# A decoder of two layers on one core: where the four-bit stage unpacks its down weights, and when it takes a batch's mean and power

## The reference

```python
w_gu = _dequant_fp4(gate_up_packed, gate_up_scales, GROUP_SIZE)   # 2*1408 x 512
w_down = _dequant_fp4(down_packed, down_scales, GROUP_SIZE)       # 512 x 1408
gate_up = jnp.einsum('bsh,oh->bso', x, w_gu)
gate, up = (gate_up[..., :I], gate_up[..., I:])
h = jax.nn.silu(gate) * up
y = jnp.einsum('bsi,hi->bsh', h, w_down)
rms = jnp.sqrt(jnp.mean(y * y, axis=-1, keepdims=True) + EPS)
return y / rms
...
x = _layernorm(x + _L1_ffn_ref(x, ...), axis=-1)
```

## Time and profile before

| | us |
|---|---|
| median of 3 runs | 1719.92 |
| lowest and highest | 1719.76 and 1720.91 |
| the profiled execution | 1719.57 |
| its span in the trace | 1717.8 |
| PE busy | 1589.3 (93%) |
| DVE busy | 1271.8 (74%) |
| POOL busy | 740.9 (43%) |
| the four-bit stage, first matmul to end of the span | 1380.03 to 1717.8 |

### The profile page before, as it was taken

How to read it: one execution, slowest core, us unless ns; L and a number is a source line. 1 busy time by engine, 2 the same in 40 slices (tenths; PEclk the granted TensorE clock), 3 DMA queues, 4 the chain that set the end, 5 groups by cost and what they waited for, 6 DMA issues and landing times. The chain is left out here.

```text
span 1717.8 us, 26427 instructions
## 1 busy us (share of the span) xinstructions
PE 1589.3 (93%) x8812; PEld 1116.1 (65%) x8812; DVE 1271.8 (74%) x2250; ACT 941.4 (55%) x1946; POOL 740.9 (43%) x718
## 2 busy tenths in 40 slices
PE   8999998999866999998999999899898989999995
PEld 5778875666524666666667566665566767777774
DVE  6466656767879899997686784876759989767574
ACT  3222225887766676766576473664544555555642
POOL 5044164777531444444531231321132257556563
PEclk9999999999988999999999999999899999999998
DMA  6200018634030000004221121121333100000000
GB/s 220 74 1 25 1 49 219 196 104 120 2 98 1 2 1 1 1 5 131 74 76 46 57 80 41 52 70 38 88 108 94 50 1 1 0 26 25 1 25 25
DMA packets 66850, 95.73 MB, mean 56 GB/s; under 512 B 12176, under 2 KB 28688, under 8 KB 66716
## 3 DMA queue, kind: packets, MB, share of 16 engines
q1 hardware_dynamic: 60044, 81.18, 15.5%
q0 software_dynamic: 6144, 12.60, 2.8%
q10 hardware_dynamic: 528, 0.26, 0.1%
HBM read 56.25 MB, written 4.19 MB: 35 GB/s over the span
## 5 line engine op out<-in xcount | busy, mean ns | idle before, releaser
L3021 PE MATMUL bank<-fp_xT,fp_weights_values 128*128 128x512 f32 x704 | 186.1, 402 | 9.6 <-DVE fp_gate L2925 8.1
L1838 ACT ACTIVATE causal_probs<-bank,causal_neg 128x512 f32<-128x512 f32 (+3 forms) x256 | 134.3, 531 | 100.9 <-DVE causal_neg L1908 66.8
L3021 PEld LDWEIGHTS bank<-fp_xT,fp_weights_values 128*128 128x128 f32 x704 | 128.5, 188 | 55.3 <-DVE fp_gate L2925 15.7
L3048 PE MATMUL bank<-fp_wd,fp_hT 128*128 128x512 f32 x528 | 133.8, 394 | 4.8 <-DVE X L2947 3.5
L2934 DVE SCALAR_TENSOR_TENSOR fp_up<-bank,fp_weights_scales,fp_up 128x512 f32<-128x512 f32 x132 | 99.1, 751 | 44.3 <-ACT fp_up L2836 37.9
L866 DVE TENSOR_REDUCE heads_neg<-bank 128x1 f32<-128x512 f32 x128 | 86.3, 676 | 50.0 <-PE bank L917 49.9
L3048 PEld LDWEIGHTS bank<-fp_wd,fp_hT 128*128 128x128 f32 x528 | 98.5, 188 | 29.2 <-issue 6.8
L1558 PE MATMUL bank<-weights_raw,ternary_qT 128*128 128x512 bf16 x448 | 107.9, 388 | 4.9 <-DVE ternary_z L1426 2.7
L835 ACT ACTIVATE heads_probs<-bank,heads_neg 128x512 f32<-128x512 f32 x128 | 88.5, 696 | 39.4 <-DVE heads_neg L866 39.4
L1232 POOL TENSOR_TENSOR ternary_z<-ternary_z 128x1024 f32<-128x1024 f32 x16 | 37.7, 2354 | 164.4 <-DVE ternary_z L1426 164.4
L2084 PE MATMUL bank<-eye,causal_probs 128*128 128x128 f32 x640 | 101.4, 283 | 5.7 <-ACT causal_pT L1820 3.6
(11 more groups left out here) (269 smaller groups left out, 4211.4 us busy)
## 6 DMA issues: line engine op xcount, KB each, us to landing
pairs_xd<-X SPq DMA_DIRECT2D x64, 128.0 KB, 2.6
pairs_cd<-in_ctx SPq DMA_DIRECT2D x64, 128.0 KB, 2.7
causal_qS<-causal_qk SPq DMA_DIRECT2D x96, 64.0 KB, 2.9
causal_qS<-causal_qk POOLq DMA_DIRECT2D x96, 64.0 KB, 2.6
causal_kS<-causal_qk SPq DMA_DIRECT2D x96, 64.0 KB, 2.7
causal_kS<-causal_qk POOLq DMA_DIRECT2D x96, 64.0 KB, 2.4
X<-in_x SPq DMA_DIRECT2D x4, 1024.0 KB, 7.8
heads_cT<-in_ctxT SPq DMA_DIRECT2D x4, 1024.0 KB, 6.0
```

Source lines behind the costliest of these rows:

```text
L1838: act.activation(probs_of(i)[:, h + one], view[:, one], ACT.Exp, bias=neg[:, G % 2, at:at + 1], accum_out=total[:, G % 2, at:at + 1]).then ...
L3021: last = pe.matmul(banks[4 + g][:], values[:, g, n % NI, of], xT[:, part, g], start=part == 0, stop=part == 1)
L3048: last = pe.matmul(banks[t][:], hT[:, n % SLOTS, a, t * P:(t + 1) * P], wd[:, c, i], start=i == 0 and k == 0, stop=i == NI - 1 and k == 2)
```

## The change

The four instructions that unpack a block of the down weights are issued elsewhere. Block 0 is unpacked ahead of step 0, block 1 behind the last `rest` of step 2, and block `n - 1` in step `n` for n = 3 to 11, between the gate's `odd` and up's `rest`. `d_highs` goes with them: 0 behind step 0's first eviction of up, 1 at the head of step 3's evictions of up, and `n - 1` behind step n's Silu. `split(0)` stands in step 0 behind the sum, `split(n - 2)` at the head of step n for n = 3 to 12. A batch's `mean` and `invert` are issued ahead of that step's `odd` and `sum`. No instruction is added or taken away on any engine.

```diff
--- before.py
+++ after.py
@@ -2799,18 +2799,20 @@
             pool.wait_ge(norm.power_set, 1)
             for n in range(STEPS):
                 b, i = divmod(n, NI)
-                if 1 <= n <= NI:
-                    split(n - 1)
+                if 3 <= n < NI + 2:
+                    split(n - 2)
+                if b and i == 2:
+                    invert(b - 1)
                 if b and i == 5:
                     root(b - 1)
                 if n == PAST_STATISTICS + 1:
                     past.norm.root(pool, 0, B * NT - 1)
                 pool.wait_ge(gate_odd, 2 * n + 2)
                 pool.tensor_tensor(gate[:, n % 2, 0], gate[:, n % 2, 0], gate[:, n % 2, 1], ALU.add).then_inc(gate_summed, 1)
+                if n == 0:
+                    split(0)
                 if n:
                     low(n - 1)
-                if b and i == 2:
-                    invert(b - 1)
                 pool.wait_ge(up_rest, 3 * n + 3)
                 pool.wait_ge(silu_ready, n + 1)
                 pool.tensor_tensor(up[:, n % 2], up[:, n % 2], gate[:, n % 2, 0], ALU.mult).then_inc(h_ready, 1)
@@ -2867,10 +2869,14 @@
                 even(n, 2)
                 if n:
                     high(n - 1)
-                if 1 <= n <= NI:
+                if n == 3:
+                    d_highs(1)
+                first(n)
+                if n == 0:
+                    d_highs(0)
+                silu(n)
+                if 3 <= n <= NI:
                     d_highs(n - 1)
-                first(n)
-                silu(n)
                 if i == 6 and b + 1 < B:
                     act.wait_ge(past.norm.normed, (b + 2) * NT)
                 if 6 <= i < 6 + NT and b + 1 < B:
@@ -2961,17 +2967,24 @@
                                       ALU.subtract, ALU.mult).then_inc(norm.normed, 1)
 
             dve.wait_ge(weights.scaled, 1)
+
+
+            d_cut(0)
+            d_weigh(0)
             for n in range(STEPS):
                 b, i = divmod(n, NI)
+                if b and i == 2:
+                    mean(b - 1)
                 odd(n, 1)
                 odd(n, 3)
-                if b and i == 2:
-                    mean(b - 1)
+                if 3 <= n <= NI:
+                    d_cut(n - 1)
+                    d_weigh(n - 1)
                 for g in range(1, NG):
                     rest(n, g)
-                if n < NI:
-                    d_cut(n)
-                    d_weigh(n)
+                if n == 2:
+                    d_cut(1)
+                    d_weigh(1)
                 if n == PAST_STATISTICS:
                     past.norm.statistics(dve, 0, B * NT - 1)
                 if n in PAST_SCALE:
```

## The result

| | before | changed |
|---|---|---|
| median | 1719.92 us | 1730.46 us |
| lowest to highest of 5 runs | 1719.41 to 1722.17 | 1729.85 to 1731.0 |
| ratio, with its 95% interval | | 1.0061 [1.0049, 1.0072] |
| the profiled execution | 1719.57 | 1729.85 |
| four-bit stage, its first matmul to the end of the span | 337.77 | 348.79 |

The change makes the kernel 10.5 us slower. The range of the prediction (1725 to 1736) holds the time, the forecast (1731.5) is 1.0 above it, and the sum (11.7) missed the difference by 1.2. The last line of the table is the sharper measure: the stages before do not have the same length in each profiled execution (this one's four-bit stage begins at 1379.31, before at 1380.03), and the stage alone is 11.02 us longer, by one profiled execution of each kernel.

A forecast was written before the change was run, and what follows sets the result against it. PE is busy 93% of the span, but DVE sets the middle steps' 7.19 us. Losses of 9.6 by E10, 3.8 and 1.7, less 3.4, give +11.7 on 1719.57; forecast median 1731.5 us, range 1725 to 1736.

The forecast's parts named there:

- at E0, the entry: End of step 0's third addition: block 0's unpacking with POOL idle makes it 1.1 us later.
- at E2: End of step 2's third addition: steps 1 and 2, without unpacking between, save about 2.5 us by then.
- at E3: End of step 3's third addition: two blocks unpacked in that step make it 0.9 us late.
- steps 4 to 10: Middle steps: DVE's unpacking meets POOL, PE waits for the split; 8.5 to 8.8 us a step, 8.7 lost.
- step 11: PE's down(9) waits for split(9), and block 10's unpacking stands ahead of the additions; 3.8 us more.
- step 12: down(10) waits for the multiply and split(10), 2.7 us behind the third addition instead of 1.0; 1.7 more.
- mean and power, 3 batches: PE's 1.16 us wait for the first add goes in each of 3 batches; -3.4 in all.
- The price that no row showed: L2907 beside POOL: nothing extra (0.42) or a whole POOL instruction as L2254 did; the second was taken.
- list of signs: Expected profile marks: L2913 about 1.4, L2907 0.8 to 1.3, PE waiting about 1 us a step, additions 8.5 apart.
- Rival 1: Only the two tensor_scalars wait for POOL, L2907 keeps 0.42; 8.05 us a step, +8.5, 1728; chance 0.17.
- Rival 2: Splits end before PE asks and steps fall to PE's 6.6 us; 1709; chance 0.07.
- Rivals 3 and 4: Losses cancel, steps 7.2 to 7.5, 1719 to 1722, chance 0.07; longer waits, L2914 meeting POOL too, 1735, chance 0.11.

The follow-up runs named there:

- x4: Changed kernel with POOL's low part of h held back in steps 3 to 11 until the block's weights are scaled; 1727.87 us.
- x8: Changed kernel with block 10 alone unpacked in its old place, behind the additions of step 10; 1727.17 us.
- x1: Kernel before the change with only mean and power moved ahead of the gate's odd and sum in batches 1 to 3; 1716.78 us.
- x3: Changed kernel with the split of block n-1 in step n, on POOL ahead of the multiply; 1724.74 us.
- x6: Changed kernel with both the split ahead of the multiply and POOL's low part of h held back; 1715.27 us.
- x2: Changed kernel with mean and power put back in their old places, so the moved unpacking alone; 1735.87 us.

## Why the prediction was right

The step marks of the changed kernel, less those of the kernel before, each from its stage's first matmul. The first three rows are readings of one running difference; the sum adds the row of E3 and those below it:

| term | predicted | measured |
|---|---|---|
| at E0, the entry | +1.1 | +0.85 |
| at E2 | -2.5 | -2.91 |
| at E3 | +0.9 | +0.50 |
| steps 4 to 10 | +8.7 | +8.27 |
| step 11 | +3.8 | +3.91 |
| step 12 | +1.7 | +1.72 |
| mean and power, 3 batches | -3.4 | -3.38 |
| sum from E3 on | +11.7 | +11.02 |

- **The bound, and what sets DVE's pace.** Right. L2901 and L2905 had shown the waits, and L2254 that a scalar_tensor_tensor with two inputs in SBUF waits too.
- **The price that no row showed**, L2907 beside POOL: a whole instruction, 1.40, as taken. The list of signs asked for 1.4 in steps 4 to 10; the walk had it clear of POOL in 9 and 10, and there it took 0.43. Rival 1 (0.42 kept) is refuted by its row, and x4 measures what it was about: 0.44 a step, as the rival had it (0.45).
- **The middle steps.** 8.43 against 8.5. Two of the signs were off, and both against the walk's own marks. PE idles 1.7 a step, where I wrote about 1: by the walk the gate begins at 7.4 and its 8 matmuls end 0.8 behind the next E, which leaves 2.0 to the split's end at 2.75 (measured: PE is there at 1.06, down begins at 2.75). The step closes the same way, as the split's end and not PE's arrival sets it. L2907 has 0.67 in steps 5 to 8, not 0.8 to 1.3: the walk had it from 2.1 to 2.85, which is 0.75.
- **Steps 11 and 12.** Right to 0.1, and x8 shows that block 10's place is where most of it comes from (4.7 of the 5.6). The lower clock behind PE's 3.44 of idle time was not foreseen. That the sum is right without it is luck: it cost nothing here only because down waited for split(10) anyway.
- **Mean and power.** Right, and shown alone by x1.
- **Where the 0.7 of the sum went:** 0.4 by E3, of which 0.25 at the entry, and 0.4 in seven steps that are 0.06 shorter, less 0.1 that step 11 took more. The medians differ by 10.5 and not 11.0; the stages before, whose length varies between executions (0.7 between the two profiled), can account for that, which is not shown for the medians.
- **Rival 2, the aim met**, had its condition right: PE must not wait for the split. x3 meets that and stays at 7.57; the 6.6 also needs L2782 out of the way (x6).
- **Rivals 3 and 4** fall by the steps of 8.43, and rival 4 also by L2920, which took 0.69 in all eleven blocks.

The Trainium skill's page "SBUF — State Buffer", section Who interferes with whom, says that issue order decides who waits at the pair of ports that Vector and GpSimd share. The runs agree: L2913 took 0.43 at the entry, where POOL was idle, and 1.40 in steps 3 to 8, and x4 brought it back to 0.43 by changing nothing but what POOL did meanwhile.

## What to carry to other kernels

Moving work on one engine moves its partners on the others: here DVE's four instructions went to a place with more room on DVE, and lost because POOL, whose instructions they wait for, was busy there and because the consumer's last step (the split) slid behind a wait that it has no part in. Look for the partner's idle gap, and put the last producer in front of the long wait, not behind it. When two arms of a loop are near each other, test the remedies together: alone they were worth 6.7 and 4.7 us here, together 16.1. Steps 6 to 8, which no stretch of lower clock disturbs, show the same: 0.86 and 0.44 a step alone, 1.78 together.

## What was not expected of the hardware

**The clock of TensorE after a stall of about two microseconds.** In the changed kernel PE idled 1.95 ahead of step 4's down and 3.44 ahead of step 12's gate. The windows behind each, and then the one behind x8's wait of 1.94 in step 4:

```profile
1409.30:1412.00 2.70, 2.62 (x11) 2.17 (x12) 2.63 (x3) 0.42 (x1) 2.53 (x2) 1.00 0.02 6
1479.70:1482.60 2.90, 2.89 (x6) 1.66 (x6) 2.15 (x3) 1.23 (x2) 1.29 (x2) 0.51 0.00 0
1411.50:1414.00 2.50, 2.22 (x6) 1.77 (x7) 2.43 (x3) 0.00 (x0) 2.50 (x3) 0.60 0.02 7
```

Behind the first the granted clock stayed at 1.00 (2.4 GHz), behind the second it was 0.51 (1.2 GHz). In x8 the program up to step 4 is the same, with a wait of 1.94 for the same split, and there the clock was 0.60, six matmuls took 2.73 instead of 1.62 and the step 1.0 more. In x2, a third kernel with the same program up to there, the wait was 1.93 and the six took 1.62 again. In x4 the clock was 0.64 behind its wait of 1.94. So in these runs a stall of that length cost itself and sometimes another microsecond, and which it was differed between profiled executions of kernels that are alike up to there; what decides it is not shown. In the changed kernel the slow stretch of step 12 cost nothing, as down waited for the split to 1483.96 anyway; in x3 and x6 such stretches ate part of what the edit gained.

**How DVE gets in between POOL's instructions.** In the changed kernel's steps 4 to 8, L2907 and L2911 each wait through one instruction of POOL whose follower is ready, and each time they get in between: they end 0.15 behind POOL's end (0.16 once), and POOL's next takes 1.33 to 1.35, where such an instruction takes 1.29 when nothing waits. L2913 ends 0.28 behind L2782, but POOL has nothing ready there, so its rows do not show who would go first. In these rows a DVE instruction that arrives waits for one POOL instruction, not for a row of them, and the next one of DVE for the next. Three short ones (0.28, 0.29 and 0.43 at the entry) so took 3.3 us.
